# A two-layer graph attention network: attention's masks and linear part moved from VectorE to TensorE, and the gelu's cubic argument in one VectorE instruction

## The reference

```python
h = _layer_norm(x, ln1_g[i], ln1_b[i])
xl = (h @ Wl + bl).reshape(n, HEADS, DIM)          # HEADS = 2, DIM = 128
xr = (h @ Wr + br).reshape(n, HEADS, DIM)
e = jax.nn.leaky_relu(xl[src] + xr[dst], NEG_SLOPE)
score = jnp.einsum('ehd,hd->eh', e, att)
smax = jax.ops.segment_max(score, dst, num_segments=n)
ex = jnp.exp(score - smax[dst])
denom = jax.ops.segment_sum(ex, dst, num_segments=n)
out = segment_sum(xl[src] * (ex / (denom[dst] + 1e-16))[..., None], dst, n) + gat_b
x = x + (out @ proj_W[i] + proj_b[i])
h = _layer_norm(x, ln2_g[i], ln2_b[i])
x = x + (jax.nn.gelu(h @ W1[i] + b1[i]) @ W2[i] + b2[i])     # MLP width 512, tanh form of gelu
```

## Time and profile before

| | |
|---|---|
| median of 3 runs | 2283.58 us (2282.32 to 2284.36) |
| the profiled execution | 2276.5 us, span 2274.8 us |
| PE busy | 1820.8 us (80%) |
| PE weight loads busy | 1285.0 us (56%) |
| VectorE busy | 1806.9 us (79%) |
| ACT busy | 1368.8 us (60%) |
| POOL busy | 1573.6 us (69%) |
| mean granted clock of TensorE | 0.933 of full speed |

### The profile page before, as it was taken

The page is one execution under the profiler, slowest core; times in us unless marked ns, Lnnn a source line. Parts: engine busy times, 40 slices in busy tenths (PEclk is TensorE's granted clock), DMA queues, the critical chain, the costliest instruction groups (busy, mean ns, idle before and its releaser), DMA issues. The chain is left out here.

```text
span 2274.8 us, 76766 instructions
## 1 busy us (share of the span) xinstructions
PE 1820.8 (80%) x22500; PEld 1285.0 (56%) x22500; DVE 1806.9 (79%) x8130; ACT 1368.8 (60%) x3471; POOL 1573.6 (69%) x1663
## 2 busy tenths in 40 slices
PE   2478888888888888888864788888878888888884
PEld 1145566665665665665642565665656656566663
DVE  6757888888888888888854788888888888888874
ACT  3444666666666666666652466666666666666664
POOL 2677777777777777777505777777777777777750
PEclk6878999999999999999976999999999999999995
DMA  4455556556556556555404555555555555555540
GB/s 105 157 158 145 150 152 157 154 150 156 150 150 161 155 146 158 149 152 153 110 23 132 150 146 147 150 152 150 150 147 155 151 149 149 148 154 151 149 109 9
DMA packets 227679, 320.66 MB, mean 141 GB/s; under 512 B 47889, under 2 KB 157574, under 8 KB 227270
## 3 DMA queue, kind: packets, MB, share of 16 engines
q0 software_dynamic: 75072, 208.30, 36.1%
q1 hardware_dynamic: 152198, 107.47, 15.9%
HBM read 295.61 MB, written 19.99 MB: 139 GB/s over the span
## 5 line engine op out<-in xcount | busy, mean ns | idle before, releaser
L973 POOL DMA_INDIRECT rows<-table,src_t x1564 | 1521.0, 973 | 495.1 <-issue 453.4
L1188 ACT ACTIVATE lz<-psum 128x512 f32<-128x512 f32 x782 | 465.6, 595 | 377.6 <-PE psum L1093 189.9
L1090 PE MATMUL psum<-ident,rows 128*128 128x128 f32 x3128 | 529.9, 294 | 56.7 <-DMA rows<-table,src_t 56.3
L1265 ACT ACTIVATE ex<-hold_s,peak 128x128 f32<-128x128 f32 x782 | 272.1, 396 | 410.4 <-DVE peak L1346 409.5
L1163 PE MATMUL psum<-rows,wgt 128*32 128x129 f32 x6256 | 260.8, 284 | 277.6 <-DVE acc L1436 277.0
L1090 PEld LDWEIGHTS psum<-ident,rows 128*128 128x128 f32 x3128 | 351.4, 146 | 210.2 <-issue 140.9
L1436 DVE SCALAR_TENSOR_TENSOR acc<-acc,keep,psum 128x129 f32 x782 | 272.5, 348 | 190.9 <-issue 115.7
L1163 PEld LDWEIGHTS psum<-rows,wgt 128*32 128x32 f32 x6256 | 159.3, 111 | 364.8 <-issue 216.9
L1074 PE MATMUL psum<-lz,att_w 128*32 128x128 f32 x6256 | 345.4, 294 | 0.0
L1093 PE MATMUL psum<-oh,xrw 96*128 96x256 bf16 x1564 | 312.9, 282 | 0.0
L1313 DVE TENSOR_SCALAR diff<-row_no,cyc_t 128x64 bf16<-128x64 f32 x1564 | 290.8, 258 | 0.0
(11 more groups left out here) (253 smaller groups left out, 2130.8 us busy)
## 6 DMA issues: line engine op xcount, KB each, us to landing
xrw<-xr_split SPq DMA_DIRECT2D x782, 48.0 KB
relb<-rel_d SPq DMA_DIRECT2D x194, 192.0 KB
rows<-table,src_t POOLq DMA_INDIRECT x1564
xr_split<-split SPq DMA_DIRECT2D x50, 192.0 KB, 1.9
table<-row SPq DMA_DIRECT2D x50, 130.0 KB, 2.0
x_mid<-x SPq DMA_DIRECT2D x25, 64.0 KB
xo<-x_mid SPq DMA_DIRECT2D x25, 64.0 KB
xo<-in_x_dram SPq DMA_DIRECT2D x24, 64.0 KB
```

The costliest lines, as they stand in the source:

```text
L973: pool.indirect_dma_start(rows[:, u % ROWS, t, :, :].rearrange("p h c -> p (h c)"), None, s["tables"][layer][0:NP, :], bass.IndirectOffset ...
L1090: pe.matmul(z[:, o:o + P], rows[:, u % ROWS, t, h, 0:D], s["ident"][:, :], is_transpose=True, start=(h == 0 and t == 0), stop=False, skip_ ...
L1188: act.activation(lz[:, u % M, :], ps[u % M][:, :], ACT.Relu).then_inc(lz_ready, 1)
L1265: m = act.activation(ex[:, (u + 1) % (2 * M), :], hold_s[:, place(u), :], ACT.Exp, bias=peak[:, place(u + 1):place(u + 1) + 1], scale=-1.0)
```

## The change

Three things change.

The masks. `diff`, `base`, `differ` and `bases` are gone. `oh` grows from 96 to 128 partitions: SP broadcasts a second list, `cyc_d` (each edge's destination modulo 32, made in `setup` and stored to memory), to the partitions 96 to 127 of `relb`, and `one_hot` compares in all 128 at once and subtracts `less` (0 in the first 96, 1 in the last 32). So the last 32 partitions hold 0 where the edge belongs to the destination and -1 elsewhere. PE multiplies `oh` by `mask_w` (zero, and -2^100 on the diagonals of the last 32 partitions), one bf16 matmul of 64 output partitions for every tile of 128 edges.

The linear part. PE adds it by a float32 matmul for every tile and head, with the row's scalar repeated 32 times as weights and the identity as the moving side, 32 output partitions each. Both stand in `score` ahead of the wait for `lz`.

The gelu. ACT squares with a scale of sqrt(0.044715), and VectorE forms (s + 1) a in one instruction.

Beside these: `oh` has three sets of buffers in place of two, its writer waits for `score_ready` in place of `z_ready`; `setup` no longer loads and transposes the destinations by tiles (`dst_d`, 7 transpositions), makes the masks' constants on GpSimd and forms the modulo on VectorE from the list by units; `row_no` is gone.

```diff
@@ setup @@
-            for t, name in ((src_d, "src"), (dst_d, "dst")):
...
+            sp.dma_start(src_d[:, 0:TJ - 1, :], g["src"][0:EFULL].rearrange("(j c p) -> c j p", c=P, p=P)
+                         ).then_inc(lists_in, 16)
...
+            sp.wait_ge(cyc_ready, 1)
+            sp.dma_start(g["cyc_d"].rearrange("(j p e) -> p j e", p=P, e=UE), cyc_h[:, :, :]).then_inc(rel_out, 16)
...
-            const(pool.iota(g["row_no0"][:, :], [[0, H], [1, W]], base=0, channel_multiplier=0,
-                            allow_small_or_imprecise_dtypes=True))
+            const(pool.memset(g["less"][0:3 * W, :], 0.0))
+            const(pool.memset(g["less"][3 * W:P, :], 1.0))
+            const(pool.memset(mask_f[:, :], 0.0))
+            for h in range(H):
+                const(pool.affine_select(out=mask_f[3 * W:P, h * W:h * W + W], in_=mask_f[3 * W:P, h * W:h * W + W],
+                                         compare_op=ALU.not_equal, fill=-BIG, base=0, pattern=[[-1, W]],
+                                         channel_multiplier=1))
+            const(pool.tensor_copy(g["mask_w"][:, :], mask_f[:, :]))
...
+            link(v.tensor_scalar(cyc_i[:, :, :], dst_u[:, :, :], PAD + W - 1, None, ALU.bitwise_and))
...
+            link(v.tensor_copy(cyc_f[:, :, :], cyc_i[:, :, :]))
+            link(v.tensor_tensor(cyc_f[:, :, :], dst_f[:, :, :], cyc_f[:, :, :], ALU.subtract))
...
+            v.scalar_tensor_tensor(cyc_h[:, :, :], cyc_f[:, :, :], neg_reg[:, 0:1], dst_f[:, :, :], ALU.mult, ALU.add
+                                   ).then_inc(cyc_ready, 1)
...
@@ edge_pass, SP @@
-                sp.dma_start(relb[:, RELS * c:RELS * c + n, :].rearrange("p k e -> p (k e)"),
+                sp.dma_start(relb[0:3 * W, RELS * c:RELS * c + n, :].rearrange("p k e -> p (k e)"),
                              s["rel_d"][i * UE:(i + n) * UE].partition_broadcast(3 * W)).then_inc(rel_in[c], 16)
+                sp.dma_start(relb[3 * W:P, RELS * c:RELS * c + n, :].rearrange("p k e -> p (k e)"),
+                             s["cyc_d"][i * UE:(i + n) * UE].partition_broadcast(W)).then_inc(rel_in[c], 16)
@@ edge_pass, PE, score @@
-                pe.wait_ge(lz_ready, u + 1)
                 if u % M == 0:
-                    pe.wait_ge(base_ready, g + 1)
                     hold(pe, held, g - 1)
-                pe.matmul(out, base[:, u % (2 * M), :, :].rearrange("p c w -> p (c w)"), s["ident"][:, :],
-                          is_transpose=True, start=True, stop=False, skip_group_check=True)
+                for t in range(K):
+                    for h in range(H):
+                        o = t * HW + h * W
+                        pe.matmul(out[o:o + W, :], rows[:, u % ROWS, t, h, D + 1:RC].to_broadcast([P, W]), s["ident"][:, :],
+                                  start=True, stop=False, skip_group_check=True)
+                for t in range(K):
+                    pe.matmul(out[t * HW:t * HW + HW, :], s["mask_w"][:, :], oh[:, u % (3 * M), t * P:t * P + P],
+                              start=False, stop=False, skip_group_check=True)
+                pe.wait_ge(lz_ready, u + 1)
@@ edge_pass, ACT @@
-                    act.activation(am2[:, :], am[t % 2][:, :], ACT.Square).then_inc(sq_ready, 1)
+                    act.activation(am2[:, :], am[t % 2][:, :], ACT.Square, scale=CUBE ** 0.5).then_inc(sq_ready, 1)
@@ edge_pass, VectorE @@
-                    m = v.tensor_scalar(oh[:, u % (2 * M), :], relb[:, u % RING, :], s["win_col"][0:3 * W, 0:1], None,
-                                        ALU.is_equal)
+                    m = v.tensor_scalar(oh[:, u % (3 * M), :], relb[:, u % RING, :], s["win_col"][:, 0:1],
+                                        s["less"][:, 0:1], ALU.is_equal, ALU.subtract)
...
-                if of_step(i):
-                    bases(i)
...
-                    hold(v, z_ready, (i - 1) * M + M)
+                    hold(v, score_ready, i - 1)
                     one_hot(i + 1)
-                    hold(v, base_ready, i)
-                    differ(i + 1)
...
-                    v.tensor_scalar(am2[:, :], am2[:, :], CUBE, 1.0, ALU.mult, ALU.add).then_inc(cub_ready, 1)
-                    v.wait_ge(cub_ready, t + 1)
                     hold(v, gelu_ready, t - 1)
-                    v.tensor_tensor(arg[t % 2][:, :], am2[:, :], am[t % 2][:, :], ALU.mult).then_inc(arg_ready, 1)
+                    v.scalar_tensor_tensor(arg[t % 2][:, :], am2[:, :], 1.0, am[t % 2][:, :], ALU.add, ALU.mult
+                                           ).then_inc(arg_ready, 1)
```

More of the change, by code:

```diff
@@ L81, in gnn @@
         win_col0 = sb("win_col0", [P, 1], F32)
-        cyc_t = sb("cyc_t", [P, TJ * P], F32)
-        row_no = sb("row_no", [P, HW], F32)
-        row_no0 = sb("row_no0", [P, HW], F32)
+        less = sb("less", [P, 1], F32)
+        mask_w = sb("mask_w", [P, HW], BF16)
         sel = sb("sel", [P, H, 3, W], F32)
@@ L168, in gnn @@
         st = dict(ident=ident, ones=ones, xs=xs, sums=sums, neg_mean=neg_mean, var=var, rstd=rstd,
-                  eps_t=eps_t, tables=tables, xr_splits=xr_splits, x_mid=x_mid, x=x, out=out, acc=acc, cyc_t=cyc_t,
-                  row_no0=row_no0, row_no=row_no, sel=sel, src_t=src_t, rel_d=rel_d, fresh=fresh, keep=keep,
+                  eps_t=eps_t, tables=tables, xr_splits=xr_splits, x_mid=x_mid, x=x, out=out, acc=acc, cyc_d=cyc_d,
+                  less=less, mask_w=mask_w, sel=sel, src_t=src_t, rel_d=rel_d, fresh=fresh, keep=keep,
                   win_col=win_col, win_col0=win_col0, at_x=at_x, at_x0=at_x0, at_s=at_s, at_s0=at_s0, at_a=at_a,
@@ L429, in _ @@
                            ).then_inc(order_ready, 1)
-            for j in range(2 * TJ):
+            for j in range(TJ):
                 act.wait_ge(turned, j + 1)
-                to = src_t[:, j, :] if j < TJ else dst_t[:, (j - TJ) * P:(j - TJ) * P + P]
-                act.copy(to, ps[3 + j % 2][:, 0:P]).then_inc(copied, 1)
+                act.copy(src_t[:, j, :], ps[3 + j % 2][:, 0:P]).then_inc(copied, 1)
             act.wait_ge(averaged, 1)
@@ L694, in reset_state @@
     pool.tensor_copy(s["win_col"][:, :], s["win_col0"][:, :]).then_inc(state, 1)
-    pool.tensor_copy(s["row_no"][:, :], s["row_no0"][:, :]).then_inc(state, 1)
     pool.tensor_copy(s["at_x"][:, :], s["at_x0"][:, :]).then_inc(state, 1)
@@ L871, in edge_pass @@
     rows = sb("rows", [P, ROWS, K, H, RC], F32)
-    relb = sb("relb", [3 * W, RING, UE], I16)
-    oh = sb("oh", [3 * W, 2 * M, UE], BF16)
+    relb = sb("relb", [P, RING, UE], I16)
+    oh = sb("oh", [P, 3 * M, UE], BF16)
     xrw = sb("xrw", [3 * W, 4 * M, HD], BF16)
     lz = sb("lz", [P, M, H * UE], F32)
-    diff = sb("diff", [P, 2 * M * K, HW], BF16)
-    base = sb("base", [P, 2 * M, K * H, W], F32)
     hold_s = sb("hold_s", [P, 4 * M, P], F32)
@@ L1347, in lowest @@
                 m.then_inc(max_ready, 1)
-            def bases(i):
-                new = of_step(i)
-                for u in new:
-                    v.wait_ge(rows_in[u % ROWS], (u // ROWS + 1) * (16 * K))
-                    v.wait_ge(diff_ready, i + 1)
-                    hold(v, score_ready, i - 1)
-                    o = u % (2 * M) * K
-                    m = v.scalar_tensor_tensor(base[:, u % (2 * M), :, :],
-                                               diff[:, o:o + K, :].rearrange("p t (h w) -> p (t h) w", h=H), BIG,
-                                               rows[:, u % ROWS, :, :, :].rearrange("p t h c -> p (t h) c"
-                                                                                   )[:, :, D + 1:RC
-                                                                                     ].to_broadcast([P, K * H, W]),
-                                               ALU.mult, ALU.add)
-                m.then_inc(base_ready, 1)
             def slots_of(b):
@@ L1385, in next_pass @@
                                 ).then_inc(moved, 1)
-                v.scalar_tensor_tensor(s["row_no"][:, :], s["step"][:, 0:1].to_broadcast([P, HW]), float(S),
-                                       s["row_no"][:, :], ALU.mult, ALU.add).then_inc(moved, 1)
             def next_tables():
-                v.wait_ge(moved, 8)
+                v.wait_ge(moved, 7)
                 v.tensor_scalar(hop[:, :], s["at_s"][:, :], SLOTS - 0.5, float(-SLOTS), ALU.is_ge, ALU.mult
```

84 lines of the change are left out of this document (32 added, 52 removed).

## The result

The changed kernel takes 2229.57 us (2228.97 to 2230.39), the kernel before, timed beside it, 2283.97 us: a ratio of 0.976 (95% interval 0.9745 to 0.9779), 54.4 us less. The direction was forecast, the size was not: 21 us were expected, and the range ended at 2246. The gain was repeated in a later comparison (0.9764). But there are chips on which the kernel before takes 2829 to 2915 us. The changed kernel itself was not run there; its variants nearest to it (without the cubic half, and with the gelu split) were, and they take 12 to 13% longer than the kernel before. Ratios are of the executions in the fast state, so they can differ by 0.001 from the quotient of two medians, and one slow execution of the kernel before, of 3910.5 us in that later comparison, is left out of them.

The account below looks back on a forecast made before the run. POOL's row gathers were taken to bound nearly everything, 40.0 us a cycle. Layer 0 -15, layer 1 -3, ends of the passes -3 and setup 0 gave -21 us, so 2283.6 became 2263 us; range 2246 to 2312.

Parts of the forecast that it names:

- PE's price: PE's added time for linear part and masks: +0.13 us first unit, +0.48 second, together +0.61 us a step.
- the bounds: Limits of PE's added time: +0.05 us a step if 64 columns stop nothing, +0.95 if masks cost 0.22 plus a stop.
- rival A: Slower: above +0.70 us a step the masks' blocks make PE the bound; 2374 us at +0.95; chance 0.24.
- The sums: PE's sums block in a step's first unit: 0.58 us before, 0.38 without its stop after the change.
- D: One-hot loses its fast form, grows 0.29 us an instruction, 4.7 us a cycle on VectorE; costs nothing, no chance of its own.
- the coupling: Layer 0: PE at 40.9 us a cycle and POOL at 40.6, taken as 41.0 together, so 15 us won.
- the term of 0.6 us a tile for stretched gathers: POOL's gathers stretched beside the gelu: 0.8 us a tile before, perhaps 0.6 with one instruction in place of two.
- The ends: Ends of the passes, where VectorE's diff, base and cubic are on the path: 1 to 2 us each, 3 us won together.
- Setup: Before the layers: at most +0.8 us for one more instruction, less 0.3 to 0.5 for each row_no copy; together 0.
- The offset: Median of timed runs 7.1 us above the profiled execution of 2276.5 us; forecast 2255.5 profiled, 2262.6 as median.
- C: No stops at 64 columns (+0.05 us a step), only POOL left at 40.5 us a cycle: 2249 us; chance 0.15.

Follow-up runs that it names:

- The masks three times: The changed kernel with each unit's two mask matmuls issued three times (result not the reference's): 2248.43 us, ratio 0.987 to the kernel before.
- The ballast: The changed kernel plus six unread VectorE instructions a step, placed and shaped as diff and base were: 2297.61 us, 1.008 of the kernel before.

## Why the prediction was right and wrong

| term | forecast | measured (spans) |
|---|---|---|
| layer 0, first to last gather | -15 | -26.2 |
| layer 1 | -3 | -10.4 |
| between the layers and the end | -3 | -8.2 |
| setup, until the first gather | 0 | -2.9 |
| sum (the spans differ by 47.5) | -21 | -47.7 |
| profiled execution against the median | 0 | -6.9 |

**Right: what bounds, and PE's price.** POOL's beat is the floor, and nearly all of the excess over it was what could be won. PE pays +0.56 us a step, with the stop from 32 to 64 columns; the bounds (+0.05 and +0.95) were closed by it, and rival A's break-even at +0.70 was not reached. Some of that is luck. The sums were put at 0.38 us and take 0.46; the masks were put at 0.22 with a stop behind them and take 0.18 twice, without one in the loads. D did no harm either: the one-hot's mean rose from 300 to 358 ns.

**Wrong: the coupling.** The first step that failed is "I take 41.0 for the two coupled". It gave PE 40.3 us a cycle, added 0.6 for waits that would remain and rounded up against POOL. Measured are 40.4 us. PE is busy 39.72 of 41.00 us and costs POOL nothing, since POOL may run ahead and VectorE is rarely late (17.4 us in all). Of the 0.6 us a cycle between forecast and measurement, 0.4 are this (8 us in layer 0), the rest are stretches. The masks three times show how far off the 0.6 was: with 1.8 us more still, layer 0 grows by 0.3 us a cycle. The ballast shows the other side: with PE as full as in the changed kernel and VectorE as full as before, layer 0 after the 110th gather takes 883.9 us, 42.1 a cycle. It was not the fuller engine that counted but the two together.

**Wrong: layer 1 and the stretches.** The second step that failed is the term of 0.6 us a tile for stretched gathers; measured is 0.28 (14 us over 50 tiles). It is all of the miss in layer 1 (40.3 us a cycle where 40.6 was forecast), and the stretches are the larger part of the gain, 25 us, where the forecast gave them 10. The reason given, one 512-column instruction in place of two, is refuted: with two of them and the masks moved, it is as small. What the forecast left out is what VectorE does around them. The gather of the earlier trace rows lies beside the end of an unbroken run of VectorE work; with VectorE at 26 of 40 us such runs should be rarer. That this is the mechanism is argued from the traces (57 of 66 gathers stretched beside the two instructions, 22 of 69 with the masks moved); the placed ballast agrees in its direction (23 us of stretch, up from 14.7), but doesn't isolate it.

**Missing: the backlog.** The ends were costed by counting instructions on the path. They hold PE's lag behind POOL as well: five projections before, two after. Of the 7.9 us between the layers, 7.7 are that (12.5 to 4.8). Two other runs agree: with the tripled masks the last projection starts 12.2 us after the last gather and the time between the layers grows by 7.0, with the placed ballast 13.3 and 8.7.

**Setup.** I left it at zero; the first gather starts 2.9 us earlier. ACT's squares begin at 29.98 us where they began at 31.59. Which removed instruction does it was not tried.

**The offset.** The forecast assumed that the median lies 7.1 us above the profiled execution after the change as before. After it is 0.6. The profile of before was a quick execution; in the later comparison the medians lie 51.3 us apart, which may be the better size of the gain.

**Of the rivals,** C named the end state (POOL alone, 40.5 us a cycle) with a wrong cause, since the stop on the way to 64 columns, which it denied, is there. Its 2249 was 19 us too slow for the terms above. The forecast gave it 0.15, because it took two nearly full engines for a bound of their own. The Trainium skill's rule on the page "TensorEngine Tiling (Array Packing)", section "Key Properties", on tiling modes that drain TensorE, holds on the way from 32 to 64 columns (0.20 us), while the way back shows no stop of that size in the loads (0.07 us).

## What to carry to other kernels

When two engines feed each other in every step and both are near the beat of a third, their load doesn't act by the larger of the two: beside PE's added work, VectorE's old load costs 35 us in layer 0 (the ballast), and loading PE with 1.8 us a cycle more beside a light VectorE costs 8. Count the backlog that a lagging engine takes into each drain as a term of its own. And before trading VectorE instructions for small matmuls, ask which engine bounds on the chips that the kernel will meet: here an added matmul cost the kernel 7 ns where POOL bounds and 42 to 53 ns where PE does, and the trade changed its sign.

## What the runs showed of the hardware

- Chips differ for one kernel by 24 to 28% (2278 to 2284 us, against 2829, 2834, 2835 and 2915 on four others), at a mean granted clock of 0.86 to 0.91 instead of 0.93 to 0.94 for the kernel before. The difference is in PE: stops, mostly of 0.3 to 1.1 us, also inside runs of equal matmuls, on average one for each 33 to 38 matmuls, and PE's busy time at 2130 us for a program of matmuls that keeps it busy 1821 us on the first chip.
- A wait of VectorE for its own last instructions, ahead of register loads, went with 0.9 us a step; without it and with another order the idle time before the accumulation was 142.6 us, not 479.5.
- A bf16 matmul of 64 output partitions and 128 columns, issued in turn to the two halves of 128 output partitions, costs 28 ns with its load (four more take 0.11 us). The loads stop for 0.20 us at the change from 32 to 64 output partitions, and are idle 0.07 us at the one back.
- A gather of 0.946 us takes up to 1.93 us in the kernel before and up to 1.55 in the changed one. Of the gathers beside the cubic's two instructions 57 of 66 were stretched before, and 22 of 69 with the masks moved.
